# New places for the steps of a transformer layer's order, and merged load semaphores, in a kernel of four attention blocks

## The reference

```python
def latent(emb, latent, Wq, bq, Wk, bk, Wv, bv, gamma, beta):      # L0 and L3
    q, k, v = emb @ Wq + bq, latent @ Wk + bk, latent @ Wv + bv
    w = softmax((q @ k.T) / sqrt(128), axis=1)                     # over the tokens
    x = w @ v + emb
    return (x - mean(x)) * rsqrt(var(x) + 1e-6) * gamma + beta

def cross(query, key, Wq, bq, Wk, bk, Wv, bv, Wo, bo):             # L1, one head of 128
    return query + softmax(Q @ K.T / sqrt(128)) @ V @ Wo + bo

def step(t, p):                                                    # L2: six layers
    tn = ln(t, norm_g, norm_b)
    t = mha(tn, tn, sa_kv, sa_q, sa_ow, sa_ob, tgt_mask) + t       # 16 heads of 64, 512 keys
    tn = ln(t, norm_g, norm_b)
    t = mha(src, tn, ca_kv, ca_q, ca_ow, ca_ob, src_mask) + t      # 16 heads, 77 keys
    tn = ln(t, pre_g, pre_b)
    return t + relu(tn @ w1 + b1) @ w2 + b2

x = latent(x, ctx, L0); x = cross(x, ctx, L1)
x = L2(src=ctx, tgt=x, masks); x = latent(x, ctx, L3)
```

## Time and profile before

| | us |
|---|---|
| runs before | 1085.88, 1084.27, 1086.04 (median 1085.88) |
| the profiled execution | 1085.62 |
| its span on the core | 1083.7 |
| TensorE busy | 1031.2 (95%) |
| ACT busy | 804.0 (74%) |
| DVE busy | 719.8 (66%) |
| POOL busy | 391.6 (36%) |

### The profile page before, as it was taken

One profiled execution on the slowest core, in us unless ns is written; L12 is line 12 of the kernel. 1 busy time (PEld: TensorE's weight loads), 2 busy tenths in 40 slices (PEclk: granted clock), 3 DMA queues, 4 the chain that ended last, 5 costly groups with the idle time before them and its releaser, 6 DMA issues.

```text
span 1083.7 us, 20569 instructions
## 1 busy us (share of the span) xinstructions
PE 1031.2 (95%) x5174; PEld 610.0 (56%) x5174; DVE 719.8 (66%) x4492; ACT 804.0 (74%) x3518; POOL 391.6 (36%) x404
## 2 busy tenths in 40 slices
PE   8899999999999999999999999999999999999984
PEld 6556555665555656555655555656555566555553
DVE  4565788556778566777765678656677755678744
ACT  4496997676998576898666798666798866699831
POOL 4143443233444233443333344223344323344420
PEclk9899999999999999999999999999999999999997
DMA  8401000003200002200002200001300000000000
GB/s 236 130 10 55 13 21 2 2 1 79 66 21 1 1 2 78 67 2 21 1 1 79 67 1 21 1 1 46 96 5 20 2 1 1 21 1 2 1 1 23
DMA packets 31802, 32.39 MB, mean 30 GB/s; under 512 B 3982, under 2 KB 27710, under 8 KB 30910
## 3 DMA queue, kind: packets, MB, share of 16 engines
q1 hardware_dynamic: 29374, 28.80, 9.5%
q10 hardware_dynamic: 2304, 2.20, 0.6%
HBM read 30.47 MB, written 0.52 MB: 29 GB/s over the span
## 4 chain that ended last, share of the span: by engine, by line
PE 85%; DVE 6%; ACT 4%; issue 3%; POOL 1%; DVEq 0%; DMA 0%; SPq 0%
PE S L1046 23%; PE T L1058 11%; PE sum L1088 10%; PE W L856 8%; PE sum L1072 7%; PE W L880 4%; PE W L911 4%; PE W L798 3%; PE W L835 3%; PE W L818 2%; PE W L813 2%; DVE Pb L1501 2%; PE W L875 2%; DVE XN L1350 2%; ACT Pb L1287 2%
## 5 line engine op out<-in xcount | busy, mean ns | idle before, releaser
L1287 ACT ACTIVATE Pb<-Pb,mn 128x128 f32<-128x128 f32 (+1 forms) x1536 | 561.1, 371 | 39.1 <-DVE mn L1501 38.7
L677 POOL TENSOR_TENSOR Pb<-Pb,rsum 128x512 f32<-128x512 f32 (+2 forms) x336 | 324.3, 969 | 610.7 <-DVE rsum L1509 610.6
L1287 ACT ACTIVATION_READ_ACCUMULATOR Pb<-Pb,mn 128x1 f32 x1536 | 295.2, 192 | 0.0
L1501 DVE CUSTOM_DVE_ANT_0 Pb<-S,late_bias 128x128 f32<-128x128 f32 x768 | 175.9, 286 | 125.9 <-PE S L1046 125.6
L1058 PEld LDWEIGHTS T<-ident,Pb 128*128 128x128 f32 (+2 forms) x1296 | 164.0, 146 | 155.4 <-issue 123.9
L1046 PE MATMUL S<-GV,XT 128*128 128x512 f32 x384 | 200.7, 610 | 1.9 <-DVE mn L1501 0.8
L1058 PE MATMUL T<-ident,Pb 128*128 128x128 f32 (+2 forms) x1296 | 197.2, 273 | 1.4 <-POOL Pb L677 1.4
L1519 DVE COPY PT<-T 128x512 f32<-128x512 f32 (+1 forms) x240 | 155.8, 649 | 59.8 <-PE T L1058 59.7
L1501 DVE CUSTOM_DVE_ANT_0 Pb<-S,cross_bias 128x77 f32<-128x77 f32 x768 | 131.8, 232 | 64.9 <-PE S L1046 62.7
L1088 PE MATMUL sum<-PT,Vc 128*128 128x512 f32 (+2 forms) x264 | 135.1, 601 | 0.2 <-DVE PT L1519 0.2
L1046 PE MATMUL S<-Gc,XT 128*128 128x462 f32 (+1 forms) x288 | 125.7, 521 | 3.5 <-DVE mn L1501 2.1
(11 more groups left out here) (175 smaller groups left out, 1061.7 us busy)
## 6 DMA issues: line engine op xcount, KB each, us to landing
sakv<-in_L_xattn_sa_kv SPq DMA_DIRECT2D x6, 1024.0 KB, 5.4
caq<-in_L_xattn_ca_q SPq DMA_DIRECT2D x6, 512.0 KB, 7.9
saq<-in_L_xattn_sa_q SPq DMA_DIRECT2D x6, 512.0 KB, 6.2
cakv<-in_L_xattn_ca_kv SPq DMA_DIRECT2D x12, 256.0 KB, 8.0
saow<-in_L_xattn_sa_ow SPq DMA_DIRECT2D x6, 512.0 KB, 4.0
w<-in_L_xattn_ff_w SPq DMA_DIRECT2D x12, 256.0 KB, 3.1
caow<-in_L_xattn_ca_ow SPq DMA_DIRECT2D x30, 96.0 KB, 3.1
GV<-in_mask_BxSxS_ik ACTq DMA_DIRECT2D x1, 1536.0 KB, 10.1
```

The costliest lines, as they stand in the source:

```text
L677: nc.gpsimd.tensor_tensor(rows, rows, r, ALU.mult).then_inc(sem(f"{unit.name}_weights"), 1)
L1287: last = nc.scalar.activation(Pb[:, s, t * w:(t + 1) * w], Pb[:, s, t * w:(t + 1) * w], ACT.Exp, bias=mn[:, s, t:t + 1], scale=-1.0, accum ...
L1501: last = nc.vector.tensor_tensor_reduce(out=Pb[:, s, cols], in0=S_ps[n % 2][:, cols], in1=row_bias, scale=1.0, scalar=3.4e38, op0=ALU.add, ...
```

## The change

It has three parts. First, the tables of ticks get new numbers. Most move by one to three ticks; the first layer's table moves most: its three groups ck/cv stood at ticks 1, 2 and 4 and its cG at 6, 7 and 9; now they stand at 6, 4 and 8 and at 11, 14 and 17.

Second, load semaphores are merged: bq, Wv and bv of L0 share one (48 for all three), the five weights of L1 share one, three columns share one, and three rows share one. Third, semaphores inside the prologue are merged (`L0_operands`, `start_norm` and the like), with the same instructions behind them. The loads themselves and their order on SP are unchanged.

```diff
-WEIGHTS0_AT = (0, 1, 3, 5, 6, 8)
+WEIGHTS0_AT = (5, 3, 7, 10, 13, 16)
...
-AFTER_S1 = (2, 3, 4, 7, 8, 9)
-AFTER_X0 = (0, 2, 3, 4, 5, 7)
-AFTER_X1 = (2, 3, 4, 4, 5, 7)
+AFTER_S1 = (2, 3, 4, 4, 5, 6)
+AFTER_X0 = (2, 2, 3, 4, 5, 7)
+AFTER_X1 = (0, 2, 3, 4, 5, 7)
...
         def loaded(s, name):
 
-            return (sem("L3_in"), 8 * 16) if s == "L3" else (sem(f"{s}_{name}_in"), 16)
+            if s == "L3":
+                return sem("L3_in"), 8 * 16
+            if s == "L1":
+                return sem("L1_in"), 5 * 16
+            if name in ("bq", "Wv", "bv"):
+                return sem("L0_values_in"), 3 * 16
+            return sem(f"{s}_{name}_in"), 16
...
-            pe.wait_ge(sem("L0_k_sb"), 1)
-            pe.wait_ge(sem("L0_wqT_sb"), 1)
+            pe.wait_ge(sem("L0_operands"), 2)
...
-            act.wait_ge(sem("L1_bv_col_in"), 16)
+            act.wait_ge(sem("columns_in"), 3 * 16)
```

More of the change, by code:

```diff
@@ L515, in load, with load_rows, load_col @@
                     sp.dma_start(place[name][:], col(v) if name in ("bq", "bk") else v).then_inc(loaded(s, name)[0], 16)
[L517 to L521, removed]
+            def load_rows(dst, s, name, done):
+                sp.dma_start(dst[:], row(a[f"{s}_xattn_{name}"])).then_inc(done, 16)
+            def load_col(dst, s, name):
+                sp.dma_start(dst[:], col(a[f"{s}_xattn_{name}"])).then_inc(sem("columns_in"), 16)
             def load_small(l, n):
@@ L643, in _ @@
               .then_inc(sem("late_bias"), 1)
-            gp.wait_ge(sem("L1_bq_in"), 16)
+            gp.wait_ge(*loaded("L1", "bq"))
             nc.gpsimd.tensor_copy(bq_wide[:], bq["L1"][:].broadcast_to([P, P])).then_inc(sem("bq_wide"), 1)
             gp.wait_ge(sem("minus_half"), 1)
[L647 to L650, removed]
+            root("start", slice(0, TB), 1)
+            root("start", slice(TB, NT), 2)
+            gp.wait_ge(sem("rows_in"), 3 * 16)
             nc.gpsimd.tensor_tensor(bo1[:], bo1[:], bet["L0"][:], ALU.add).then_inc(sem("bo_beta"), 1)
-            gp.wait_ge(sem("L0_gamma_in"), 16)
             gp.wait_ge(sem("bo_beta"), 1)
-            gp.wait_ge(sem("L0_norm"), B)
+            gp.wait_ge(sem("start_norm"), B)
             for b in range(B):
@@ L664, in _ @@
             for b in range(B):
-                root("first", slice(b * TB, (b + 1) * TB), b + 1)
+                root("start", slice(b * TB, (b + 1) * TB), B + b + 1)
             def decoder(unit, l):
@@ L1203, in _ @@
             act.wait_ge(sem("L0_k"), 1)
[L1204 removed]
+            key_copy("L0", S_ps[1]).then_inc(sem("L0_operands"), 1)
             load_mask(slice(KEYS, T), "late_mask_in")
             act.wait_ge(sem("L0_wqT"), 1)
[L1207 removed]
+            nc.scalar.activation(wqTo["L0"][:], sum_ps[:, 0:P], ACT.Copy).then_inc(sem("L0_operands"), 1)
             act.wait_ge(sem("A_turned"), 1)
@@ L1220, in _ @@
             act.wait_ge(sem("L1_k"), 1)
-            key_copy("L1", S_ps[1]).then_inc(sem("L1_k_sb"), 1)
+            key_copy("L1", S_ps[1]).then_inc(sem("L1_operands"), 1)
             act.wait_ge(sem("L1_wqT"), 1)
-            nc.scalar.activation(wqTo["L1"][:], sum_ps[:, 0:P], ACT.Copy).then_inc(sem("L1_wqT_sb"), 1)
+            nc.scalar.activation(wqTo["L1"][:], sum_ps[:, 0:P], ACT.Copy).then_inc(sem("L1_operands"), 1)
             act.wait_ge(sem("L1_G"), 1)
@@ L1433, in _ @@
                 nc.vector.tensor_tensor(X[:, batch(b), :], tiles(T_ps[b][:]), X[:, batch(b), :], ALU.add)
-                normalise(0, batch(b), XN, EPS_LATENT, "L0", b + 1)
+                normalise(0, batch(b), XN, EPS_LATENT, "start", b + 1)
                 if b == 1:
-                    normalise(2, batch(0), XN, EPS_LATENT, "L0", 1)
-                normalise(1, batch(b), XN, EPS_LATENT, "L0", b + 1)
+                    normalise(2, batch(0), XN, EPS_LATENT, "start", 1)
+                normalise(1, batch(b), XN, EPS_LATENT, "start", b + 1)
             def latent_residual(b):
@@ L1458, in second_least @@
                 last.then_inc(sem("L1_masked"), 1)
-            normalise(2, batch(1), XN, EPS_LATENT, "L0", 2)
+            normalise(2, batch(1), XN, EPS_LATENT, "start", 2)
             dve.wait_ge(sem("pads_zero"), 1)
@@ L1469, in _ @@
             second_least(1)
-            normalise(0, batch(0), XN, EPS_DEC, "first", 1)
-            normalise(1, batch(0), XN, EPS_DEC, "first", 1)
+            normalise(0, batch(0), XN, EPS_DEC, "start", B + 1)
+            normalise(1, batch(0), XN, EPS_DEC, "start", B + 1)
             dve.wait_ge(sem("bad_sum"), 1)
@@ L1477, in _ @@
             nc.vector.tensor_scalar(cross_bias[:], cross_bias[:].bitcast(I32), 0, BIG, ALU.is_equal, ALU.mult)
-            normalise(2, batch(0), XN, EPS_DEC, "first", 1)
+            normalise(2, batch(0), XN, EPS_DEC, "start", B + 1)
             latent_residual(1)
-            normalise(0, batch(1), XN, EPS_DEC, "first", 2)
-            normalise(1, batch(1), XN, EPS_DEC, "first", 2)
-            normalise(2, batch(1), XN, EPS_DEC, "first", 2)
+            normalise(0, batch(1), XN, EPS_DEC, "start", B + 2)
+            normalise(1, batch(1), XN, EPS_DEC, "start", B + 2)
+            normalise(2, batch(1), XN, EPS_DEC, "start", B + 2)
             def decoder(unit, l):
```

47 lines of the change are left out of this document (22 added, 25 removed).

## The result

The new kernel takes 1073.76 us (median of 4 runs, 1072.97 to 1076.72) against 1085.08 us of the one before: ratio 0.990, 95% interval 0.9878 to 0.9923, so 11.3 us faster. The profiled run took 1074.49 us.

The account below looks back on a forecast made before the run. TensorE was taken as the bound, busy 1031.2 of 1083.7 us. 1085.62 - 7.5 - 3.5 + 2.1 = 1076.7, plus 0.26 for the median gave 1077.0 us; range 1073.3 to 1081.7, with 48% on 1075 to 1079.

Parts of the forecast that it names:

- First layer: First decoder layer's start: new order removes long brackets and slow clock, leaving 2.9 us of new idle time; 7.5 us gained.
- Rival A: New start: the clock stays or falls low somewhere, so 4.05 us come back, 1081 us; 10%.
- Semaphore: Prologue: the matmul of bq now also waits for bv, landed at 8.4 us; 2.1 us lost.
- rival C: Prologue: bv lands early enough in most runs, 1074.9 us; 6%.
- Boundary: Five layer boundaries: last Gc products fill k's wait (3.1 us) and shorten the scores' second wait (0.4); 3.5 us gained.
- Norm: Batch 1's norm behind the self-attention, six layers, made without its pause: net 0, bounds -0.5 to +0.6 us a layer.
- Rival E: Behind the self-attention, six layers: DVE becomes the bound, 3 us a layer or 18 in all slower, 1095 us; 5%.
- ACT's lead: Each layer: ACT gets some 2 us ahead, so evicting oT behind exponentials costs nothing; without it 0.7 us a layer.
- The wait of 1.19 us: Ahead of a cross product in each layer: a DVE queue (norm, kTc, vTb) that stays.
- The other tables: Other steps moved by a tick: they cross no bracket and change nothing.
- The clock: TensorE's granted clock: 1.00 from 34 to 1050 us, since the new start's holes are at most 1.1 us.
- rival D: Tail: gap shrinks from 3.9 to 2.7 us; if the clock then holds, 2.5 us more gained, 1074.5 us; 12%.

Follow-up runs that it names:

- b_first: Kernel before with only the new tables of the first layer's cross products (WEIGHTS0_AT, CV0_AT); 1077.74 us, ratio 0.9943.
- a_split: New kernel with bq, Wv and bv of L0 on semaphores of their own again; 1071.94 us, ratio 0.9889.
- b_s1: Kernel before with the new AFTER_S1 alone (norm of batch 1 behind the self-attention in one piece); 1084.63 us, ratio 0.9999.
- a_s1: New kernel with the old AFTER_S1 (norm of batch 1 has its pause of three ticks again); 1080.50 us, ratio 0.9960.
- a_x0: New kernel with the old AFTER_X0 (ACT evicts oT ahead of a chunk of exponentials again); 1073.28 us, ratio 0.9897.
- fill2: New kernel with split semaphores and idle matmuls in TensorE's waits, about half as many as in fill; 1068.73 us, ratio 0.9856.
- cv36: New kernel with split semaphores and each next layer's second cross product one tick later; 1073.48 us, ratio 0.9902.
- fill: New kernel with split semaphores and idle matmuls on the identity where TensorE waits; 1074.30 us, ratio 0.9906.
- fill3: fill2 with five tables as before the change (CV_AT, SELF1_AT, SELF0_AT, AFTER_S0, AFTER_X1); 1067.63 us, ratio 0.9838.
- b_sem: Kernel before with one shared semaphore for bq, Wv and bv of L0 and nothing else; 1086.97 us, ratio 1.0025.

## Where the prediction was right and where not

1077.0 us was forecast, 1073.76 measured: faster as said, but under the 1075 to 1079 that had 48%, and only 0.5 us above the lower end of the range. That range does not follow from the bounds of the terms, as the prediction says it does: added up, they reach from 1071.4 to 1084.1. The profiled run took 2.2 us less than the sum of 1076.7.

- **First layer.** Right in mechanism and nearly in size: holes of 0.85, 1.1, 0.65 and 0.3 us forecast, 0.96, 1.11, 0.48 and none seen; first scores at 43.3 and 43.03; full clock from 34 to 100 us. 8.4 us in the place of 7.5, in a pair of profiles that is at the high end (6.9 to 8.4, b_first). Rival A (the clock falls in the new start) did not come in this run, but in the profiled run of a_split, at 35 to 39 us, for 1.2 us. The stretch of 0.65 us of work in 2 us, which kept full clock and was the argument against it, was one case and no rule.
- **Semaphore.** Right: 8.42 us forecast for L732, 8.44 seen; 2.1 and 1.9 us. The row on the very load (4.2 us) was the right one to take, so rival C did not come. The Trainium skill (DMA: Bandwidth & Descriptors, Anatomy of one DMA) has about 2.0 us as the fixed cost, in a section on loads that GpSimd issues. This load is issued by SyncE while others are under way, and took 4.2 us; taken over to it, the figure does not agree with the trace.
- **Boundary.** Right: 3.5 and 3.4, measured alone. That the second wait would go was wrong: 0.16 and 0.17 us stay, only the two of 0.32 shrink to 0.16.
- **Norm.** The step "Net 0" failed. It is right for the edit alone (b_s1). But I weighed it apart from WEIGHTS_AT, in which one step moves by three ticks into the very stretch where the replay showed the new waits, and dismissed the rest as "moved by a tick". In company it gives 3.7 us (0.6 a layer, the sixth layer's also without company). That is the largest error of the sum. Rival E had the right sign for the DVE (0.44 to 0.62 us of wait at XN in each layer) but not the size: root and statistics stay hidden.
- **ACT's lead** is shown by a_s1, with a price of 0.57 us a layer if it is missing. The eviction's move costs nothing with it, as said. Its size was off: with the eviction in its old place (a_x0) ACT waits 2.61 us ahead of it, where it waited 1.36 before, so the lead is 1.25 us and not 2; 0.7 was needed.

```profile
167.34 0.69 ACT L1319 ACTIVATE oT<-sum,small 128x512 f32<-128x512 f32 x1 [2.61 <-PE sum L1090]
```

- **The wait of 1.19 us** did not stay but grew to 1.44, for no loss: it is the slack of a point set by the DVE.
- **The other tables** at nothing: they cost 1.0 us, 0.2 a layer. Which of the five does was not tried.
- **The clock.** "1.00 from 34 to 1050" was wrong in the profiled run at 848 us (1.7 us), and rival D did not come: the gap in the tail shrank from 3.88 to 2.52 us (2.7 forecast), and the clock fell all the same. Two more gaps, of 0.87 and 0.78 us, stand ahead of it in the new order. Its price was forecast as 2.5 us; fill2, which holds the clock there, gains 2.2.

So four errors, +3.7 and +0.9 against -1.0 and -1.7, and small ones left 2.2 us. The good total owes something to their opposite signs.

## What to carry to other kernels

Moves in one schedule are not to be priced one by one: write down the waits that each opens, and look which other move puts work there. Where an engine's start at some point is fixed by another engine's queue, the idle time ahead of it is slack, and reordering the first engine only renames who waits; cv36 even lost by it. Before small gains are hunted, make the clock steady: fillers in known holes gave 3.2 us here (a_split to fill2) and cut the spread of the runs from 1.5 to 0.4 us. They must be shorter than their hole: the longer ones of fill lost 2.4 us.

## What the hardware showed that was not expected

The clock falls in the same hole in some runs and not in others. The fifth of the waits of 1.44 us in the new kernel, in windows and then in TensorE's rows:

```profile
844.00:848.00 4.00, 2.47 (x22) 1.00 0.00 0
848.00:852.00 4.00, 4.00 (x20) 0.58 0.00 0
```

```profile
848.62 1.38 PE L1048 MATMUL S<-Gc,XT 128*128 128x308 f32 x2
...
850.64 2.60 PE L884 MATMUL W<-XT,w 128*128 128x512 f32 x4
```

and the same place in a_x0, behind a wait of 1.18 us:

```profile
848.54 0.79 PE L1048 MATMUL S<-Gc,XT 128*128 128x308 f32 x2
...
849.60 1.88 PE L884 MATMUL W<-XT,w 128*128 128x512 f32 x4
```

The four holes of 1.40 to 1.44 us before it left the clock at 1.00 in the same run. In a_split and b_first the decoder starts with the same hole of 0.96 us, at 35.12 and 35.14; the first two windows are a_split's, the others b_first's:

```profile
32.00:36.00 4.00, 2.71 (x17) 0.88 0.45 122
36.00:40.00 4.00, 3.83 (x24) 0.69 0.61 164
```

```profile
32.00:36.00 4.00, 2.68 (x21) 1.00 0.43 121
36.00:40.00 4.00, 2.88 (x31) 1.00 0.62 164
```

So a hole is not by its length alone a loss or none; it carries a chance of losing 1.2 to 1.7 us (what the lead lost at these two places). In the profiled runs of fill, fill2 and fill3, which lack most of these holes, the clock is at 1.00 until TensorE's last matmul, and the timed runs of each lie within 0.2 to 0.7 us. What decides in a single run is open.

The second is the start. The two score matmuls of the first attention have a granted clock of 1.00 beside them in every profile, but not one duration. The same line in the new kernel and in b_sem (min/median/max in ns):

```profile
L952 PE MATMUL T<-XT,L0G x4: 1057/1057/1134, 11.1 to 13.7; 128*77 128x512 f32 x4
```

```profile
L953 PE MATMUL T<-XT,L0G x4: 592/772/1138, 11.0 to 13.1; 128*77 128x512 f32 x4
```

TensorE works at the lower of its two levels until some point that differs between runs. In a_split the first short matmul of this line starts at 11.5 us, in b_sem at 12.7. In the new kernel all four are long, and the fillers behind them are long too until about 15.7:

```profile
14.56 1.66 PE L926 MATMUL W<-ident 128*128 128x128 f32 x8
```

In b_sem the same eight take 1.04 us, and the stretch of the four takes 2.74 us there and 3.69 here. The column of the clock doesn't show it. It moved the decoder's start by some 0.9 us, which is why the profiled b_sem lost 0.84 us and not 1.9, and the leads above are counted from the decoder's start where this matters.
